# A graph attention layer on one core: VectorE takes two of eight batches of column copies, POOL waits one chunk less far ahead in two chunks, ScalarE copies z after p

## The reference

```python
h = relu(layernorm(x))                                    # [N, 64]
h_edge = ((h[src] + bond) @ W).reshape(-1, 2, 64)         # two heads
h_node = (h @ W).reshape(-1, 2, 64)
s = leaky_relu(einsum(h_edge, attn_l) + einsum(h_node, attn_r)[dst], 0.2)
alpha = softmax of s over the edges with the same dst
ft = segment_sum(h_edge * alpha[..., None], dst)          # [N, 2, 64]
z = relu(batchnorm(ft.mean(axis=1)))                      # over the nodes
return x + z
```

## Time and profile before

| | |
|---|---|
| time, median of 3 (us) | 1906.42 (1903.43 to 1906.96) |
| profiled execution: time, span (us) | 1907.24, 1905.5 |
| mean granted TensorE clock, share of full speed | 0.667 |
| busy share: PE, DVE, ACT, POOL | 53%, 60%, 55%, 73% |
| chain that ended last: POOL, issue | 63%, 22% |

### The profile page before, as it was taken

The page is one execution under the profiler, slowest core; times in us unless marked ns, Lnnn a source line. Parts: engine busy times, 40 slices in busy tenths (PEclk is TensorE's granted clock), DMA queues, the critical chain, the costliest instruction groups (busy, mean ns, idle before and its releaser), DMA issues.

```text
span 1905.5 us, 44809 instructions
## 1 busy us (share of the span) xinstructions
PE 1017.8 (53%) x6780; PEld 768.6 (40%) x6780; DVE 1134.7 (60%) x3350; ACT 1052.9 (55%) x8687; POOL 1399.3 (73%) x1487
## 2 busy tenths in 40 slices
PE   2626656446545644555465455445554654655556
PEld 2515444335334433443343344334433433433345
DVE  7878755556455556555554655556555556555665
ACT  2420366556565665666565665656665665656542
POOL 7777767777777777777777777777777777777770
PEclk9857767666666766676666667666766666666666
DMA  8643232232223223222322332232223223322335
GB/s 234 174 97 95 61 93 63 63 96 64 63 66 94 63 63 89 71 63 63 97 63 63 78 81 63 63 97 63 64 63 96 63 63 83 77 63 63 97 71 138
DMA packets 77495, 156.47 MB, mean 82 GB/s; under 512 B 34276, under 2 KB 38896, under 8 KB 70544
## 3 DMA queue, kind: packets, MB, share of 16 engines
q0 software_dynamic: 47264, 49.90, 16.1%
q1 hardware_dynamic: 28818, 99.91, 16.0%
q10 hardware_dynamic: 1112, 3.73, 0.8%
HBM read 142.19 MB, written 9.80 MB: 80 GB/s over the span
## 4 chain that ended last, share of the span: by engine, by line
POOL 63%; issue 22%; PE 6%; DVE 5%; DMA 2%; ACT 1%; ACTq 1%; DVEq 0%; SPq 0%
POOL work L686 63%; PE po L1073 2%; PE p_s L937 1%; PE p_s L974 1%; DMA er_run<-er_tab,er_idx 1%; DMA acc<-in_x 1%; ACT cols L831 1%; ACTq L457 1%; DMA h_tab<-acc 1%; PE pt L926 1%; PE pt L961 0%; PE p_s L1003 0%; POOL er_run L700 0%; DVE acc L1250 0%; DVE acc L1248 0%
## 5 line engine op out<-in xcount | busy, mean ns | idle before, releaser
L686 POOL DMA_INDIRECT work<-h_tab,srcI x1406 | 1328.3, 945 | 438.1 <-issue 427.4
L831 ACT ACTIVATE cols<-acc 32x2 f32 x8448 | 939.0, 201 | 524.7 <-issue 503.0
L1199 DVE COPY elh<-work 128x16 f32<-128x16 f32 (+2 forms) x222 | 41.8, 199 | 599.2 <-DMA work<-h_tab,srcI 595.3
L1073 PE MATMUL po<-scaled,work 128*65 128x64 f32 x3104 | 287.1, 278 | 56.4 <-issue 53.3
L1073 PEld LDWEIGHTS po<-scaled,work 128*65 128x65 f32 x3104 | 281.8, 194 | 73.9 <-issue 73.0
L961 PE MATMUL pt<-ident,work 128*128 128x128 f32 x784 | 192.2, 390 | 119.4 <-DVE work L1204 119.3
L1011 PE MATMUL p_s<-ident,elh 128*32 128x128 f32 x196 | 50.2, 409 | 306.0 <-DVE elh L1199 306.0
L961 PEld LDWEIGHTS pt<-ident,work 128*128 128x128 f32 x784 | 138.7, 200 | 149.0 <-DVE work L1204 126.1
L1544 DVE TENSOR_TENSOR acc<-acc,po 65x64 f32 x776 | 168.3, 217 | 27.5 <-PE po L1073 1.3
L974 PE MATMUL p_s<-work,wpair 128*32 128x256 f32 x784 | 181.2, 385 | 1.6 <-DVEq L1154 1.6
L1011 PEld LDWEIGHTS p_s<-ident,elh 128*32 128x32 f32 x196 | 25.5, 154 | 317.2 <-DVE elh L1199 313.0
(11 more groups left out here) (218 smaller groups left out, 1235.1 us busy)
## 6 DMA issues: line engine op xcount, KB each, us to landing
row_tile<-h_tab SPq DMA_DIRECT2D x3392, 0.3 KB
work<-in_ea_t SPq DMA_DIRECT2D x49, 1024.0 KB
ohT_i<-in_dst_n SPq DMA_DIRECT2D x49, 512.0 KB
work<-h_tab,srcI POOLq DMA_INDIRECT x1406
acc<-hT_tab SPq DMA_DIRECT2D x2, 1562.5 KB, 14.0
h_tab<-acc SPq DMA_DIRECT2D x1, 2887.5 KB
work<-in_x SPq DMA_DIRECT2D x1, 2800.0 KB
out<-work SPq DMA_DIRECT2D x5, 448.0 KB
```

The lines of the kernel that those rows point to most:

```text
L686: pool.indirect_dma_start(out=row, out_offset=None, in_=x if c < RAW else h_tab, in_offset=bass.IndirectOffsetOnAxis(ap=srcI[:, c, j, g:g ...
L831: copied = nc.scalar.activation(view(cols[0:HALF, n % COL_BUFS, 0, i:i + 1], [[P, H]]), view(acc[CP:P, 0, bass.ds(r, 1)], [[NACC, H]]), AC ...
L1073: m = mm(bank[0:F1, w0:w0 + H * WIN], edge[c % 2][:, j, g, :], scaled[:, j * CG + g, :, :].rearrange("p h w -> p (h w)"), start=(j == 0), ...
L1199: copied = v.tensor_copy(elh[:, q, js, :, g0:g1], rows_h[:, :, :, F:FH].rearrange("p j g h -> p j h g"))
```

## The change

Three things change. First, every chunk from 5 on has both tiles of group 12 as column tiles, so 88 in all instead of 66. A round is now eight batches per chunk: ACT copies the first six, DVE the other two, from chunk 3 to chunk 46. DVE's batches come one after each half of the additions, before the third quarter of the next chunk and at the end of the chunk. DVE has its own semaphore, `cols_dve_ok`, for which PE (`turn` of the fourth quarter), ACT (last chunk) and SP (end) wait too. Second, POOL's wait for `p_turned` in chunks 5 and 48 is for one less: p of chunk c - 2. Third, ACT copies z behind p instead of before `fexp`, except in the last chunk. The clearing of the unused place in `gat` is written so that it covers the new tile.

```diff
-COL_BATCHES = 6
+COL_BATCHES = (6, 2)
+COL_ROUND = sum(COL_BATCHES)
...
-    return [(j, COL_G) for j in range(EPP if c % 2 == 0 else 1)]
+    return [(j, COL_G) for j in range(EPP)]
...
+def col_batches_upto(c):
+
+    n = cols_upto(c) * P // COL_BATCH
+    by_dve = n // COL_ROUND * COL_BATCHES[1] + max(0, n % COL_ROUND - COL_BATCHES[0])
+    return n - by_dve, by_dve
...
-            sp.wait_ge(cols_ok, cols_upto(NCH - 1) * P // COL_BATCH)
+            sp.wait_ge(cols_ok, col_batches_upto(NCH - 1)[0])
+            sp.wait_ge(cols_dve_ok, col_batches_upto(NCH - 1)[1])
...
-                    pool.wait_ge(p_turned, c)
+                    pool.wait_ge(p_turned, c - (c == LEAD or last))
...
-                b0 = COL_BATCHES * (c - COL_FIRST + 2)
-                for cc, j, r0 in col_batches[b0:b0 + COL_BATCHES]:
+                b0 = COL_ROUND * (c - COL_FIRST + 2)
+                for cc, j, r0 in col_batches[b0:b0 + COL_BATCHES[0]]:
...
                 if c == NCH - 1:
+                    act.wait_ge(cols_dve_ok, col_batches_upto(c)[1])
                     z_keep(NZ - 5, zT_made, zT_ok)
                 if c == NCH - 1:
                     z_keep(NZ - 4, zT_made, zT_ok)
-                else:
-                    for b in z_seen(c):
-                        z_keep_halves(b)
...
                 nc.scalar.activation(pT[:, :], sdif[:, :], ACT.Exp).then_inc(p_ok, 1)
+                if c < NCH - 1:
+                    for b in z_seen(c):
+                        z_keep_halves(b)
...
-                    pe.wait_ge(cols_ok, cols_upto(c) * P // COL_BATCH)
+                    pe.wait_ge(cols_ok, col_batches_upto(c)[0])
+                    pe.wait_ge(cols_dve_ok, col_batches_upto(c)[1])
...
+            def load_cols(c, i):
+
+                if c == COL_FIRST - 2:
+                    dve.wait_ge(cols_table_in, 32)
+                b0 = COL_ROUND * (c - COL_FIRST + 2) + COL_BATCHES[0] + i
+                for cc, j, r0 in col_batches[b0:b0 + 1]:
+                    n = cols_upto(cc - 1) + j
+                    if n >= COL_BUFS:
+                        dve.wait_ge(cols_read, n - COL_BUFS + 1)
+                    for i, r in enumerate(col_regs(cc, j * P + r0, j * P + r0 + COL_BATCH, ENG.DVE), r0):
+                        copied = v.tensor_copy(view(cols[0:HALF, n % COL_BUFS, 0, i:i + 1], [[P, H]]),
+                                               view(acc[CP:P, 0, bass.ds(r, 1)], [[NACC, H]]))
+                    copied.then_inc(cols_dve_ok, 1)
...
                         else:
                             added.then_inc(sums_added, 1)
+                    if i < COL_BATCHES[1] and COL_FIRST - 2 <= c < NCH - 2:
+                        load_cols(c, i)
                     if g1 == 8 and RAW <= c + 1 < NCH:
                         make_e(c + 1, 2 if c + 1 < NCH - 1 else 1)
```

More of the change, by code:

```diff
@@ L325, in gnn_kernel @@
         cols_ok = sem("cols_ok")
+        cols_dve_ok = sem("cols_dve_ok")
         cols_read = sem("cols_read")
@@ L453, in far_regs, with col_regs @@
                 skip_runtime_bounds_check_because="src and dst hold numbers of nodes")[1]
-        def col_regs(c, o0, o1):
+        col_batches = [(c, j, r0) for c in range(NCH) for j, g in col_tiles(c) for r0 in range(0, P, COL_BATCH)]
+        assert len(col_batches) <= COL_ROUND * (NCH - COL_FIRST)
+        def col_regs(c, o0, o1, which):
             return nc.values_load_multi_w_load_instructions(
-                coffs[c:c + 1, o0:o1], engines=[mybir.EngineType.Activation], min_val=0, max_val=N - 1,
+                coffs[c:c + 1, o0:o1], engines=[which], min_val=0, max_val=N - 1,
                 skip_runtime_bounds_check_because="src and dst hold numbers of nodes")[1]
@@ L818, in z_keep_halves @@
                 kept.then_inc(zT_ok, 1)
-            col_batches = [(c, j, r0) for c in range(NCH) for j, g in col_tiles(c) for r0 in range(0, P, COL_BATCH)]
-            assert len(col_batches) <= COL_BATCHES * (NCH - COL_FIRST)
             def load_cols(c):
-                b0 = COL_BATCHES * (c - COL_FIRST + 2)
-                for cc, j, r0 in col_batches[b0:b0 + COL_BATCHES]:
+                b0 = COL_ROUND * (c - COL_FIRST + 2)
+                for cc, j, r0 in col_batches[b0:b0 + COL_BATCHES[0]]:
                     n = cols_upto(cc - 1) + j
@@ L829, in load_cols @@
                         act.wait_ge(cols_read, n - COL_BUFS + 1)
-                    for i, r in enumerate(col_regs(cc, j * P + r0, j * P + r0 + COL_BATCH), r0):
+                    for i, r in enumerate(col_regs(cc, j * P + r0, j * P + r0 + COL_BATCH, ENG.Activation), r0):
                         copied = nc.scalar.activation(view(cols[0:HALF, n % COL_BUFS, 0, i:i + 1], [[P, H]]),
@@ L1206, in make_e @@
                 added.then_inc(e_ok, 1)
-                if k == NQ - 1 and c in (COL_FIRST - 2, COL_FIRST - 1):
+                fresh = [jg for jg in col_tiles(c + 2) if jg not in col_tiles(c)] if k == NQ - 1 and c + 2 < NCH else []
+                if fresh:
                     dve.wait_ge(e_ok, NQ * (c + 1))
                     dve.wait_ge(elh_ok, NQ * (c + 1))
-                    for j, g in col_tiles(c + 2):
+                    for j, g in fresh:
                         step(v.memset(gat[q][:, j, g, :], 0.0))
```

## The result

The changed kernel takes 1899.47 us (median of 12 runs, 1897.19 to 1902.19), the kernel before 1905.55 us (12 runs, 1903.35 to 1906.96): ratio 0.9969 with a 95% interval of 0.9962 to 0.9977. So it is 6 us faster, where 22 were forecast. The 22 gathers are gone, and most of their 27.5 us has been given back.

A forecast was written before the change was run, and what follows sets the result against it. POOL's gathers at 1.25 us each were taken to bound the kernel. Start -3.6, middle -26.2, slower gathers +1.2 and end +6.6 sum to -22.0 us from 1906.42: 1884.5 us, 8-in-10 range 1877 to 1902.

The forecast's parts named there:

- Gathers removed: Odd chunks 5 to 47 each lose one POOL gather of 1.25 us: 22 gathers, 27.5 us gained.
- One DVE batch, b: Time of one DVE batch, a load of 32 registers and 32 copies: 5.7 us, bounds 3.7 and 10.2.
- Steady chunks: Batches make DVE's fourth quarter 2.0 to 3.3 us late; POOL has 7.5 us to spare, so price 0.
- Threshold: DVE becomes the bound at 6.4 us per batch; beyond it every 0.1 us more costs 9 us.
- third case: Rival: batches of 6.2 to 6.5 us, or gathers 20 to 60 ns longer: 1889 to 1903 us; chance 12%.
- the 1.0 us per chunk for DVE's wait for p: Term of the threshold: DVE's wait for p in each chunk, which no gap covers then, 1.0 us.
- the 22.9: DVE's work in one steady chunk of the kernel before, without its waits for gathers: 22.9 us.
- Start: POOL's pause in chunk 5 goes, about two thirds returns in chunk 6, restart at 281.1: 3.6 us gained.
- End: In chunk 47 lateness of 0.9 us and a DVE batch of 5.7 lie on the final chain: 6.6 us lost.
- The looser waits: POOL's waits for p in chunks 5 and 48: 6.27 us of chunk 5's pause goes, chunk 48's frees nothing.
- z behind p: ACT's z copies (0.55 us) placed behind p: up to 0.55 us helped in chunk 4, elsewhere priced at nothing.
- The rival on the port: DVE's copies hold POOL back, each gather under a batch growing 156 ns: 37 us, 1920 us; chance 4%.

The follow-up runs named there:

- b_pace: The kernel before with only POOL's two looser waits for p (chunks 5 and 48): 1901.49 us, ratio 0.9965 to the kernel before.
- e_c16: The changed kernel with 16 register-address copies per DVE batch instead of 32, plus one plain copy of 16 columns: 1883.77 us, ratio 0.9872.
- e_static3: The changed kernel with DVE's batch copies reading fixed columns, which also left no DVE register load: 1878.34 us, ratio 0.984.
- e_stop: The changed kernel without DVE batches in chunks 45 and 46, one gather more: 1893.13 us, ratio 0.9906.
- e_up: The changed kernel with POOL's waits for p in chunks 5 and 48 as before the change: 1902.3 us, ratio 0.9967.
- e_uz3: The changed kernel with ACT copying z ahead of p again, as before the change, in an ordinary set: 1900.38 us, ratio 0.997.

## Why the prediction was wrong

Two steps failed: the price of a batch, and in the steady chunks the lateness that was to cost nothing. The second also undid the start.

**Gathers removed: right.** 1384 at 1.25 us. Their mean is 945.4 ns against 944.7 (1308.4 / 1384, 1328.3 / 1406), 0.9 us in all; b_pace, without any copies of DVE, has 946.4, so that isn't clear of the scatter.

**One DVE batch, b: failed.** 5.7 us was taken, with "likely 5.3 to 6.4"; it is 6.50 on average. The load of 32 registers, scaled up from 4 and 16, was 2.15 and is 2.27 (+0.1). The copies were priced at ACT's 107 ns because the register operations of both engines took 46 ns. But the earlier trace rows belongs to additions, not to a copy with a register address; for that DVE needs 57 ns of them and comes every 126 ns: 32 x 0.019 = +0.6 us. Pauses and single longer distances add 0.2 us, the last copy's own length 0.1. The 0.2 us for stretched copies wasn't needed: a copy of up to 421 ns doesn't delay those behind it. Apart from the 41 pauses no copy starts more than 160 ns after the one before it.

**Steady chunks, "Lateness of 3 us costs nothing ... Price 0": failed.** The fourth quarter was to be 2.0 to 3.3 us late, and POOL had 7.5 us to spare. The chain from the quarter to POOL is right. In the chunk shown above, whose fourth quarter begins at 935.00, POOL waits at position 17:

```profile
946.34 0.94 POOL L699 DMA_INDIRECT work<-h_tab,srcI  x1 [0.93 <-PE p_m L1065]
```

It goes on 11.3 us after the fourth quarter began, against 11.1. The spare is even larger, since POOL asks for p 18 gathers after the chunk's last one and not 17: 22.5 - 2.5 - 11.3 = 8.7 us. But the lateness is 7.4 to 9.7 us, around this spare, so POOL stands in 22 of 40 chunks. With b = 6.50 the prediction's own sum of gaps gives 1.9 + 1.7 = 3.6 us, or 4.9; so a longer batch explains only part of the lateness, and where the rest comes from stays open.

**Threshold: near the mark, in part by luck.** The prediction set the turn at b = 6.4, with each 0.1 us beyond costing 9 us. At 6.50 its formula gives 1884.4 + 0.7 x 6 + 9 = 1897.6 us, 8.8 us gained where 6.1 were; that is its third case, 1889 to 1903, to which it gave 12%. But the 1.0 us per chunk for DVE's wait for p is mis-sized. The earlier trace rows has 0.19 us there; the rest of the 0.95 is the first quarter, which the 22.9 hold already, and measured is 6.3 / 40 = 0.16. Without it the turn would be at (36.7 - 22.9 - 0.2) / 2 = 6.8, and b lies below it. The middle lost its 9.2 us through POOL's 22 waits, before DVE's own work came up to POOL's. So the loss sets in gradually ahead of the threshold. With b well below it the sum as a whole holds: at about 4.5 us (e_c16: 2.27 + 2.25) it gives -4.9 - 26.2 + 4.5 = -26.6, measured 1.28% = -24.4 (+-3); at 2.5 (e_static3) -28.6, measured 1.6% = -30.5 (+-3).

**Start: failed with the same step.** POOL did restart where forecast (281.65 against 281.1, a gain of 3.05 us against 284.70), but DVE's mask of chunk 6 came 4.9 us later than before: it lagged 7.9 us further behind POOL. The start was counted at POOL alone, and the lag that DVE kept was priced at nothing.

**End: the size nearly right, its reason too small.** +4.3 measured from the mask of chunk 46 against 5.4. But e_stop won 12 us from chunk 45 on, not the 6.6: 7.9 in chunk 45, 3.7 in chunk 46, 0.3 behind it. A carried lag is paid there too.

**The looser waits: wrong by the company they keep.** Two thirds of the removed pause were seen to come back, and 2.4 us credited. In the change nothing of it is seen (e_up, within some 2.7 us; 0.2 us by the masks of chunks 5 and 7), alone they give 6.7 us (b_pace).

**z behind p: right**, nothing that can be measured (e_uz3).

**The rival on the port: rightly refused.** The gathers are 945 ns at the median in the changed kernel as before, and the copies at fixed addresses show that it isn't the copies' limit either. The page SBUF — State Buffer of the Trainium skill (section Who interferes with whom) has a DVE copy in a two-port mode and a GpSimd operation exclude one another; whether these copies are in that mode no run shows. DVE's rows agree with it for the last third of a gather only: of the 272 copies over 300 ns in the changed kernel all began 0.51 to 0.64 us into a gather, and 271 ended within 0.02 us of its end. But 1475 of the 2816 copies end in the midst of a gather, so the two don't exclude one another for its whole length. POOL's rows show nothing of it, and the pace of neither follows.

The page Perfetto Trace Analysis (section Optimizing Scalar/DVE Operations) of the Trainium skill gives a DVE instruction on SBUF an overhead of about 60 ns. With fixed addresses the runs come near to it (73 ns); with an address from a register, 126, DVE is slower than ScalarE at 107, against the order that the page gives.

## What to carry to other kernels

When work is moved onto an engine's slack, work out the threshold at which it becomes the bound, and if the price lies near the threshold within its own uncertainty, measure that price first: here a batch of 6.5 us instead of 5.7 went with the loss of most of the gain, and batches of 4.5 and 2.5 us brought it back. Don't take the mean of a chunk for the threshold: two engines with nearly the same work per chunk stand for one another before either is full. Then edits elsewhere may be worth nothing, and lateness that was free is carried to the end. Spare the places that have no slack: leaving the batches out of the first and last two chunks, for two more gathers, brought over four times the gain of the whole change.

## What the runs showed of the hardware

- A copy with its source address in a register costs the DVE queue more than the ACT queue: 57 ns of register operations and 126 ns from copy to copy, against 46 and 107 ns. With a fixed address DVE's come every 73 ns.
- DVE's load of 32 registers takes 2.27 us at the median, ACT's 1.98.
- 32x2 copies of DVE beside POOL's gathers are now and then stretched to 300 to 421 ns, and then end with the gather (271 of 272 within 0.02 us); neither the distance of the copies nor the 945 ns of the gathers changes.
- In two sets all kernels took 1.6 times as long, with single copies as short as ever and more idle time before them (769.7 us on DVE against 206.0 in the changed kernel); the cause is open. The kernel with z ahead of p, 0.3% faster than before in ordinary runs, was then some 2% slower (1.0224 and 1.0252).
